# A stencil split in a local part, finished early, and time neighbours, added by transfers

## The reference, cut to what matters

```
x1 = x  + pooled attention over time (masked softmax)                 # stage one
x2 = x1 + zX*(channel neighbours - 2*x1) + zY*(time neighbours - 2*x1) + zR*x1*(1-x1)
   = x1*(1 - 2*(zX+zY) + zR - zR*x1) + zX*(left+right) + zY*(before+after)
x3 = x2 + LayerNorm(x2 + relu(x2 @ Wd + bd) @ Wu + bu) * g + b        # adapter
y  = x3 + LayerNorm((gelu(soma) * sigmoid(temporal)) @ Wout) * gamma + beta
```

## Time and profile before

| what | value |
|---|---|
| median of three runs | 774.7 us (771.69 to 777.08) |
| the profiled execution, its own time | 777.66 us |
| its span, first to last instruction | 775.8 us |
| mean granted clock of TensorE | 0.944 of full |
| busy: PE, DVE, ACT, POOL | 685.9, 552.1, 332.5, 213.3 us |
| moved by DMA | 82.62 MB, mean 106 GB/s |

### The profile page before, as it was taken

One profiled execution on the slowest core, in us unless ns is written; L12 is line 12 of the kernel. 1 busy time (PEld: TensorE's weight loads), 2 busy tenths in 40 slices (PEclk: granted clock), 3 DMA queues, 4 the chain that ended last, 5 costly groups with the idle time before them and its releaser, 6 DMA issues.

```text
span 775.8 us, 7905 instructions
## 1 busy us (share of the span) xinstructions
PE 685.9 (88%) x2808; PEld 503.2 (65%) x2808; DVE 552.1 (71%) x736; ACT 332.5 (43%) x694; POOL 213.3 (27%) x219
## 2 busy tenths in 40 slices
PE   4979398479999979997999799979997999899986
PEld 2445154237778757875787578757775777577874
DVE  3545265674985997599659975987599759875964
ACT  1241136214357235723572356235623661465244
POOL 5004212742324312431243124213421342031001
PEclk9989689689999989998999999989999999899999
DMA  7965858497305170517041805270427050405001
GB/s 223 303 221 175 259 143 266 146 274 228 55 0 109 58 160 1 109 58 160 0 109 58 159 2 108 72 145 1 110 80 138 0 109 1 55 1 109 0 1 55
DMA packets 49829, 82.62 MB, mean 106 GB/s; under 512 B 8176, under 2 KB 10224, under 8 KB 49790
## 3 DMA queue, kind: packets, MB, share of 16 engines
q1 hardware_dynamic: 33630, 56.93, 21.3%
q0 software_dynamic: 12672, 25.17, 20.0%
q10 hardware_dynamic: 3488, 0.01, 0.3%
HBM read 65.31 MB, written 16.79 MB: 106 GB/s over the span
## 4 chain that ended last, share of the span: by engine, by line
PE 57%; DVE 18%; issue 8%; ACT 6%; DMA 5%; POOL 4%; SPq 1%; POOLq 0%; DVEq 0%; ACTq 0%
PE bank L1019 13%; PE bank L1021 13%; PE bank L1020 13%; POOL wide L534 4%; PE bank L1059 4%; PE bank L1075 3%; DVE hb L1444 3%; DVE tr L1465 3%; PE bank L922 3%; DVE xr L1375 2%; DMA wg_l_f<-in_wg 2%; PE bank L1015 2%; PE bank L1084 2%; DVE tr L1459 2%; ACT wide L702 2%
## 5 line engine op out<-in xcount | busy, mean ns | idle before, releaser
L1367 DVE SCALAR_TENSOR_TENSOR nb<-nb,coef,wide 128x2048 f32<-128x2048 f32 x8 | 38.9, 4867 | 44.4 <-POOL wide L534 30.3
L1465 DVE TENSOR_TENSOR_SCAN tr<-alpha,carry,tr 128x512 f32<-128x512 f32 x48 | 58.9, 1268 | 0.0
L584 POOL TENSOR_TENSOR rs_a<-ss_a,consts 128x1 f32<-128x1 f32 x32 | 15.9, 498 | 131.7 <-ACT hb L721 131.6
L1019 PE MATMUL bank<-xh,wg_l 128*128 128x512 f32 x128 | 52.1, 407 | 0.0
L1019 PE MATMUL bank<-th,wg_l 128*128 128x512 f32 x128 | 52.0, 406 | 0.0
L1021 PE MATMUL bank<-xh,wg_h 128*128 128x512 f32 x128 | 50.2, 392 | 0.0
L1021 PE MATMUL bank<-th,wg_h 128*128 128x512 f32 x128 | 50.1, 391 | 0.0
L1020 PE MATMUL bank<-xl,wg_h 128*128 128x512 f32 x128 | 50.1, 391 | 0.0
L1020 PE MATMUL bank<-tl,wg_h 128*128 128x512 f32 x128 | 49.9, 390 | 0.0
L1459 DVE SCALAR_TENSOR_TENSOR tr<-wgb,blend_w,mod 128x512 f32<-128x512 f32 x64 | 45.3, 749 | 3.8 <-ACT mod L747 2.9
L570 POOL DMA_DIRECT2D xr<-rows_scratch x16 | 23.5, 1466 | 77.5 <-PE bank L1084 55.9
(11 more groups left out here) (238 smaller groups left out, 1994.9 us busy)
## 6 DMA issues: line engine op xcount, KB each, us to landing
xr<-rows_scratch POOLq DMA_DIRECT2D x16, 1024.0 KB, 10.8
xb<-in_x SPq DMA_DIRECT2D x8, 1024.0 KB, 14.5
x_scratch<-xb SPq DMA_DIRECT2D x8, 1024.0 KB, 6.0
nb<-x_scratch SPq DMA_DIRECT2D x8, 1024.0 KB, 5.5
nb<-x_scratch POOLq DMA_DIRECT2D x8, 1024.0 KB, 9.3
x1s<-x_scratch SPq DMA_DIRECT2D x7, 1024.0 KB, 5.6
result<-xr SPq DMA_DIRECT2D x7, 1024.0 KB, 4.3
xb<-in_xT SPq DMA_DIRECT2D x3, 1024.0 KB, 10.4
```

What stands on the lines that cost most here:

```text
L1019: pe.matmul(acc, wl, xh_, start=start, stop=False)
L1367: ve.scalar_tensor_tensor(flat(nb[:]), flat(nb[:]), coef[:, ZY, b:b + 1], flat(wide[:]), ALU.mult, ALU.add).then_inc(mix_t, 1)
L1465: ve.tensor_tensor_scan(t[:, d], alpha[:, 1 + d:2 + d].broadcast_to([P, GN]), t[:, d], 0.0 if first else carry[:, k, 1 + d:2 + d], ALU.mul ...
```

## The change

The stencil is split by linearity. In **stage one**, each of the eight blocks n of 512 steps gets its local part finished as soon as its x1 is there: ScalarE `mix_local(n)` makes the factor in a buffer `local_of(n)`, VectorE `by_local(n)` multiplies it by x1 (this was POOL's `local`), POOL `channels(n)` makes left+right in one buffer `side`, and VectorE `stencil(n)` adds zX times `side`. ScalarE `scale_beside(n)` then multiplies x1 by zY in place, and `store_beside(n)` stores that with one row more on each side; `store_local(n)` stores the local part (the program stores it for blocks 2 to 7, and blocks 0 and 1 stay in `xr`). In **stage two** nothing is mixed. `load_x2(q)` loads the local part, two buffers in turn, and the two time neighbours are added onto it by two accumulating transfers of the POOL queue, `add_before(q)` and `add_after(q)`, the second waiting for the first. `x2_transposes(q)` now waits for `after_add`. `times` is gone.

Moved along with it: 

- `xT` of batch 1 goes into buffers of the gate weights and is loaded with x of batch 1 and `wn1` right behind the first loads, with no wait; the two halves of `wg` are loaded behind `hid_mm` 8, and `wg_hi(0)` no longer stands between `tanh(1, 2)` and `tanh(1, 3)` on ScalarE. It stands behind the evictions of `probT`.
- `pooled` of batch 0 uses three banks in turn, not two. `x2_transposes(0)` stands behind `pooled(1, 1)` (was behind `pooled(0, 12)`), `down(0)` behind `pooled(1, 3)`, `up(0)` behind `pooled(1, 5)`, `x3_transposes(0)` behind `pooled(1, 9)` (was behind `pooled(1, 7)`); `replicate(1)` stands behind `pooled(0, 13)`.
- ScalarE in stage one, after: `tanh(1,1)`, `scale_beside(0)`, `mix_local(1)`, `tanh(1,2)`, `tanh(1,3)`, `scale_beside(1)`, `mix_local(2)`, the softmax's `block_exps(1)` and `prob_exps(1)`, `sums_raw(1)`, `wn1` high, `scale_beside(2)`, `sums_hi(1)`, `bw_evict` and `probT_evict` of batch 1, `mix_local(3)`, `wg_hi(0)`, `scale_beside(3)`, `x2_evict(0)`, `wg_hi(1)`, `relu(0)`, and on as in the diff.
- VectorE in stage one, after: `x1(0, 7)`, `by_local(0)`, `stencil(0)`, `params_a`, `read_scores(1, 0)`, `x1(0, 8)`, `params_b`, `read_scores(1, 1)`, `x1(0, 9)`, `by_local(1)`, `stencil(1)`, `read_scores(1, 2)`, `x1(0, 10)`, `x1(0, 11)`, `read_scores(1, 3)`, `softmax_in(1)`, `x1(0, 12)`, `x1(0, 13)`, `by_local(2)`, `normalise_out(1)`, `x1(0, 14)`, `stencil(2)`, `normalise(1)`, `sums_low(1)`, `x1(0, 15)`, `x1(1, 0)`, `x1(1, 1)`, `by_local(3)`, `stencil(3)`, `x1(1, 2..5)`, `y_sum(0, 0..3)`, `x1(1, 6)`, `x1(1, 7)`, `ln_weigh(0, 0..3)` with `x1(1, 8)` and `x1(1, 9)`, `ln_apply(0, 0..3)`, and on as in the diff.
- In `front(g)` the products CTX of a column block come ahead of PRE. `mod` is halved per d, behind `sigmoid_gate(g, 0)`.
- In group 0, `weight_hi(2)` (`wo`) and `weight_hi(1)` (`wt`) and their low halves on POOL follow within the group; `soma_in(0, 0)` still waits for `w2_lo` 2.

The core of the diff:

```diff
+
+        def x2_of(q):
+            return xr[:, q] if q < 2 else (x2b0, x2b1)[q % 2][:]
...
+            xt_slot = [[xts[:, 0], xts[:, 1], xts[:, 2], as_slot(probT[:])],
+                       [wg_raw[:, 0:KE], wg_raw[:, KE:], wg_st[:, 0:KE], wg_st[:, KE:]]]
+            side = as_tiles(xts[:, 2])
+
+            def local_of(n):
+                return xr[:, n] if n < 2 else as_tiles(xts[:, n % 2])
...
+                    def store_beside(n):
+                        b, j = n // NG, n % NG
+                        sp.wait_ge(beside_done, n + 1)
+                        done = beside_out[b][j]
...
+                    def store_local(n):
+                        sp.wait_ge(local_done, n + 1)
+                        sp.dma_start(local_rows(n), local_of(n)).then_inc(local_out[n], 16)
+
+                    def load_x2(q):
+                        if q == 2:
+                            beside_landed(sp, 0, 0)
+                        elif q == 3:
+                            sp.wait_ge(x1_done, B * NT)
+                            sp.wait_ge(local_done, GROUPS)
+                            sp.wait_ge(beside_done, GROUPS)
                         else:
-                            sp.wait_ge(mix_v, q)
-                            sp.wait_ge(chan, 3 * q)
-                        sp.dma_start(x1s[:], rows_of_x1(b, j, 0)).then_inc(x1s_in, 16)
+                            sp.wait_ge(x3_done, GT * (q - 1))
+                        sp.wait_ge(local_out[q], 16)
+                        sp.dma_start(x2_of(q), local_rows(q)).then_inc(x2_in, 16)
...
+                    def channels(n):
+                        xg = x1_of(n)
+                        po.wait_ge(x1_done, GT * (n + 1))
+                        if n:
+                            po.wait_ge(local_done, n)
+                        po.tensor_tensor(side[:, :, 1:E - 1], xg[:, :, 0:E - 2], xg[:, :, 2:E], ALU.add)\
+                          .then_inc(chan, 1)
+                        po.tensor_scalar(side[:, :, 0:1], xg[:, :, 1:2], 2.0, None, ALU.mult).then_inc(chan, 1)
+                        po.tensor_scalar(side[:, :, E - 1:E], xg[:, :, E - 2:E - 1], 2.0, None, ALU.mult)\
+                          .then_inc(chan, 1)
+
+                    def add_before(q):
+                        b, j = q // NG, q % NG
+                        if q < 2:
+                            po.wait_ge(local_done, q + 1)
                         else:
-                            po.wait_ge(x1s_in, 16 * q)
-                        if q == 1:
-                            po.wait_ge(masks_set, S_MASKS)
-                        elif q > 1:
-                            po.wait_ge(o_out, 16 * (q - 1))
-                        po.tensor_tensor(s[:, :, 1:E - 1], xg[:, :, 0:E - 2], xg[:, :, 2:E], ALU.add)\
-                          .then_inc(chan, 1)
-                        po.tensor_scalar(s[:, :, 0:1], xg[:, :, 1:2], 2.0, None, ALU.mult).then_inc(chan, 1)
-                        po.tensor_scalar(s[:, :, E - 1:E], xg[:, :, E - 2:E - 1], 2.0, None, ALU.mult)\
-                          .then_inc(chan, 1)
+                            po.wait_ge(x2_in, 16 * (q - 1))
+                        beside_landed(po, b, j - 1)
+                        beside_landed(po, b, j)
+                        po.dma_start(x2_of(q), beside_rows(b, j, -1), accum_op=ALU.add).then_inc(before_add, 16)
 
...
                     def add_after(q):
                         b, j = q // NG, q % NG
-                        po.wait_ge(nb_in, 16 * (q + 1))
-                        x1_landed(po, b, j)
-                        x1_landed(po, b, j + 1)
-                        po.dma_start(nb[:], rows_of_x1(b, j, 1), accum_op=ALU.add).then_inc(nb_sum, 16)
+                        po.wait_ge(before_add, 16 * (q + 1))
+                        beside_landed(po, b, j + 1)
+                        po.dma_start(x2_of(q), beside_rows(b, j, 1), accum_op=ALU.add).then_inc(after_add, 16)
...
-                    local(0)
                     channels(0)
+                    channels(1)
+                    add_before(0)
+                    channels(2)
                     add_after(0)
-                    weight_low(0, wg_h[:, 0:KE], wg_l[:, 0:KE], wg_st[:, 0:KE])
+                    weight_low(0, wn1_h[:], wn1_l[:], wn1_st[:])
+                    channels(3)
+                    add_before(1)
                     add_up_bias(0)
-                    weight_low(1, wg_h[:, KE:], wg_l[:, KE:], wg_st[:, KE:])
+                    weight_low(1, wg_h[:, 0:KE], wg_l[:, 0:KE], wg_st[:, 0:KE])
                     add_after(1)
-                    weight_low(2, wn1_h[:], wn1_l[:], wn1_st[:])
+                    weight_low(2, wg_h[:, KE:], wg_l[:, KE:], wg_st[:, KE:])
+                    channels(4)
                     for c in range(GT):
                         rstd(ln_ss, ss_a, EPSILON, rs_a, c, ln_p, ln_rs, c)
-                    local(1)
-                    channels(1)
+                    channels(5)
                     add_shift(0)
-                    weight2_low(1, wo_h[:], wo_l[:], wo_st[:])
-                    add_after(2)
-                    weight2_low(2, ws_h[:], ws_l[:], ws_st[:])
+                    channels(6)
+                    channels(7)
+                    weight2_low(1, ws_h[:], ws_l[:], ws_st[:])
...
+                        if g + 2 < GROUPS:
+                            add_before(g + 2)
+                            if g == 0:
+                                weight2_low(2, wo_h[:], wo_l[:], wo_st[:])
+                            add_after(g + 2)
                         if g < LAST:
                             add_up_bias(g + 1)
+                            if g == 0:
+                                weight2_low(3, wt_h[:], wt_l[:], wt_st[:])
                             for c in range(GT):
...
+                    def mix_local(n):
+                        b = n // NG
+                        act.wait_ge(x1_done, GT * (n + 1))
+                        if n < 2:
+                            act.wait_ge(masks_set, S_MASKS)
+                        elif n >= 4:
+                            act.wait_ge(local_out[n - 2], 16)
+                        act.activation(local_of(n), x1_of(n), ACT.Identity, bias=coef[:, MID, b:b + 1],
+                                       scale=coef[:, NEG_ZR, b:b + 1]).then_inc(mix_u, 1)
+
+                    def scale_beside(n):
+                        b = n // NG
+                        act.wait_ge(mix_v, n + 1)
+                        act.wait_ge(chan, 3 * (n + 1))
+                        act.activation(x1_of(n), x1_of(n), ACT.Identity, scale=coef[:, ZY, b:b + 1])\
+                           .then_inc(beside_done, 1)
...
+                    mix_local(4)
                     for c in range(GT):
                         ln_moments(0, c)
-                    wg_hi(2, wn1_h[:], wn1_st[:])
-                    mix_local(1)
+                    scale_beside(4)
+                    mix_local(5)
                     act.wait_ge(params_set, S_PARAMS)
-                    for j in range(NG):
-                        x1_landed(act, 0, j)
+                    beside_landed(act, 0, 3)
                     x3_evict(0)
-                    weight_hi(2, wo_h[:], wo_st[:])
+                    scale_beside(5)
+                    mix_local(6)
+                    mix_local(7)
+                    scale_beside(6)
                     weight_hi(0, ws_h[:], ws_st[:])
+                    scale_beside(7)
...
-                        if g and adapted:
-                            mix_local(g + 1)
                         n1_gelu(g)
-                        mod_sigmoid(g)
                         keep_ctx(g, 0)
                         sigmoid_gate(g, 0)
-                        add_half(g)
+                        mod_sigmoid(g)
...
+                                pe.wait_ge(x3T_hi, KE * g + 3)
                             elif k == 1:
-                                pe.wait_ge(o_done, GT * g)
+                                pe.wait_ge(n1_act, g + 1)
                             elif k == 2:
                                 pe.wait_ge(x3T_hi, KE * g + KE)
                             else:
+                                pe.wait_ge(ctx_scan, KE * g + 1)
+                            by_x3(g, bank[CTX[k]][:], wg_h, wg_l, KE, chunk(k)).then_inc(ctx_mm, 1)
+                            if k == 0:
+                                pe.wait_ge(x3T_hi, KE * g + 2)
+                            elif k == 1 and g > 0:
+                                pe.wait_ge(o_done, GT * g)
+                            elif k == 3:
                                 pe.wait_ge(pre_add, KE * g + 1)
                             by_x3(g, bank[PRE[k]][:], wg_h, wg_l, 0, chunk(k)).then_inc(pre_mm, 1)
-                            if k == 0:
-                                pe.wait_ge(x3T_hi, KE * g + 3)
-                            elif k == 3:
-                                pe.wait_ge(ctx_scan, KE * g + 1)
```

(57 more changed lines are left out.)

326 lines of the change are left out of this document (144 added, 182 removed).

## The result

The changed kernel takes 743.8 us (median of 4 runs), the kernel before 773.2 in the same job: ratio 0.962, interval 0.957 to 0.967. The forecast was 736 in a range of 724 to 755. The profiled execution took 746.6 us with a span of 744.8, against 775.8 before.

A forecast was written before the change was run, and what follows sets the result against it. Stage two was held bound by the mixing chain ahead of logits(g, 0), then TensorE; stage one by a string of waits. 777.66 - 43.1 - 1 + 0 + 5.5 = 739.1, or 736 us on the medians' scale, range 724 to 755.

The forecast's parts named there:

- Stage two: Groups 1 to 6, freed of mixing, go from 77.13 to 69.94 us each, 43.1 us less in all.
- B: Rival: stage two keeps a wait of 2 us per group, set by the VectorE chain; +18, 754 us; chance 0.08.
- The exchange of CTX and PRE: In front(g), the first scan can start some 2.7 us earlier, but the add still waits for PRE; costed at nothing.
- The two transfers: POOL's accumulating transfers in stage two: cost nothing with their lead of a group, up to 27 us per group without.
- Last group: Group 7, with mod halved per d: 1 us gained, bounds 0 to 1.5.
- Stage one: Start of front(0) stays at about 171.5 against 172.31: no change, bounds -8 and +13.
- The walk: Some forty steps of stage one followed in the new order, ending with x1(1, 15) at about 171.5.
- Tail and group 0: Last mixing steps, 13.3 us in series on VectorE, make TensorE stand 5 to 7 us before mod: +5.5, bounds 0 and 12.
- A: Rival: stage one grows through the shared side, the port and ScalarE as middleman; +26, 762 us; chance 0.12.
- C: Rival: each stage-one block becomes a closed ring of 12.85 us, making the kernel slower at 789 us; chance 0.03.
- D: Rival: stage one comes out 12 us shorter, the 11.0 and 13.1 us waits both gone; 724 us; chance 0.10.

The follow-up runs named there:

- logits2: Kernel before, on VectorE times(g+1) moved behind logits(g, 1) and logits(g, 2) ahead of traces(g, 1) and trace_lo(g, 0), mixing kept in stage two: 733.6 us, ratio 0.950.
- ctx_first: Kernel before with only CTX made ahead of PRE in front(g): 772.6 us, ratio 1.000.
- swap_back: Changed kernel with PRE ahead of CTX again in front: 748.1 us, ratio 0.968.
- adds_late: Changed kernel with both accumulating transfers of block g+1 issued at the head of group g, without their lead of a group: 744.4 us, ratio 0.963.
- evict_bias: Changed kernel with the order of evict_first and, on POOL, add_up_bias(0) ahead of add_before(1): 742.4 us, ratio 0.960.
- ws_low_late: Changed kernel with POOL's weight2_low(1), the low half of wsoma, waiting until stencil(7) is done: 744.3 us, ratio 0.964.
- evict_first: Changed kernel, ScalarE doing x2_evict(0) ahead of wg_hi(0) and scale_beside(3), and x3_evict(0) ahead of scale_beside(4) and mix_local(5): 741.9 us, ratio 0.959.
- mod_later: The evict_first kernel with the two mod products of group 0 behind PRE[2] in place of PRE[0]: 752.9 us, ratio 0.974.

## Why the prediction was right, and which terms were off

The forecast of 736 us was 7.8 short of the measured 743.8: stage two came out 2 us better, stage one 4 to 6 worse, the tail and group 0 5 worse.

**Stage two, forecast -43.1, measured -45.1.** Mechanism and size held. The floor that I read from group 0, 69.94 us, is 69.62; TensorE is busy in all of it at clock 1.00. B (a wait stays) is excluded by that row.

**What I had not drawn from it.** I named the chain ahead of `logits(g, 0)` as the limit and took the removal of the mixing as its cure. `logits2` shows that the mixing can stay where it was: two changes of order on VectorE bring the same 69.62. So the 4.7 us of VectorE per group were not the cost; the cost was their place ahead of two deadlines, `logits(g, 0)` and `logits(g, 2)`. In the kernel before, `times` took 5.59 us ahead of the first, and all scans of the group stood behind it.

**The exchange of CTX and PRE, forecast 0.** Right in the kernel before (`ctx_first`, ratio 1.000), and in groups 1 to 6. It has a value outside them: undone in the changed kernel it costs 4 us (`swap_back`), of which 2.5 are placed, in group 0 and the last group; put into `logits2` it gives 3.6.

**The two transfers, forecast 0 with their lead, up to 27 without.** The 0 held. The 27 was wrong by all of it: `adds_late` costs nothing. I had counted the string from the load, which can stay early, and left out the 24 us between POOL's first issue and the transposes.

**Last group, forecast -1, measured -0.7.**

**Stage one, forecast 0 (-8 to +13), measured +4.3, like for like +6.** This step was mis-sized. The walk got the front half: first `probT` eviction 105.55 (forecast 104), end of `scale_beside(3)` 116.9 (117.6). The adapter came later than walked:

```profile
119.95 1.28 POOL L578 DMA_DIRECT2D xr<-rows_scratch  x1 [3.85 <-PE bank L1081]
135.75 0.69 DVE L1452 SCALAR_TENSOR_TENSOR tr<-bank,xr 128x512 f32<-128x512 f32 x1 [6.75 <-DMA xr<-rows_scratch]
152.91 2.00 ACT L719 ACTIVATE xb<-xb,coef 128x2048 f32<-128x2048 f32 x1 [10.81 <-DVE xts L1404]
156.81 0.67 ACT L749 ACTIVATE soma<-bank,shift_cols 128x512 f32<-128x512 f32 x1
```

The bias row landed at 135.7 in place of 131, so `ln_apply(0)` ended at 150.7 in place of 144, and ScalarE stood in `scale_beside(4)` until 152.91 and reached `x3_evict(0)` at 156.8 in place of 150.5. With both of ScalarE's stands removed `front(0)` starts at 170.6 and the kernel is 2 us faster, so they carry part of it. The last `x1` ended at 176.4 (forecast 171.5), and TensorE stood 8.8 us for it ahead of `front(0)`, where I had the 3.5 of before. Why the bias row landed late is in part shown: issued ahead of `add_before(1)` it takes 10.2 us (`evict_bias`).

**Tail and group 0, forecast +5.5 (0 to 12), measured +10.4.** The mechanism held and a term was missing. TensorE waits 6.27 us for `wn_rep` (forecast 5 to 7) with the slow clock behind it: the four `mod` products ran at a granted clock of 0.50, the 1.2 GHz level, in 3.75 us in place of 1.88:

```profile
188.00:194.25 6.25, 0.00 (x0) 0.03 (x1) 6.22 (x4) 3.14 (x3) 4.80 (x2) 0.90 1.01 349
194.25:198.50 4.25, 4.25 (x6) 2.09 (x7) 2.72 (x4) 2.67 (x5) 0.00 (x0) 0.50 1.03 158
```

`mod` came 17.6 us behind `front(0)` against 9.9 before, that is 7.7 of the 10.4: the wait, and 1.4 since the 36 products ahead of it took 11.3 us at a mean granted clock of 0.73, against 9.9 at 0.83 before. The other 2.7 are from `mod` to `x3_transposes(1)`, 51.79 against 49.06; the slow `mod` is 1.9 of it. The Trainium skill's rule (SBUF — State Buffer, "SBUF: two separate sides") that a VectorE instruction with two SBUF inputs and a GpSimd one that reads SBUF exclude each other for a whole instruction is borne out in both directions in the tail, 6.60 us for a VectorE step of 2.35 and 5.50 for a POOL step of 3.6.

What I left out is that POOL's weight half lands in the tail too: over 4 us more in series, on `stencil(7)` here, on the copies in `ws_low_late` and `evict_first`. From the start of `by_local(6)` at 176.3 to the end of the copies at 194.1 the tail took 17.8 us, not the 13.3 that I added up. That the wait still came out at its forecast is luck: I had the 36 products at 8.2 us, and their slow clock hid 3.1 of the 4.5.

A (762) and C (789) did not come: `front(0)` moved by 4 to 6 us, not by 26 or more. I take it that the `pooled` products fill the time between the blocks; no run tests that. D (724) did not come: the wait of 13.1 us is gone and that of 11.0 is down to 5.3, but TensorE now also stands 8.8, 6.6, 5.4 and 5.3 us in stage one.

**Slips in the working.** None changes the forecast. ScalarE's added work is six `mix_local` and eight `scale_beside` of 2.1 us, 29.4 and not 27. The row of 20.88 us is that of group 7; group 0 has 252.21 - 231.29 = 20.92. The DMA share of the group's row is 0.37, not 0.38.

## What to carry to other kernels

When the engine that should be the floor waits in every turn of a loop, list what its supplier does between its last free moment and that delivery, and ask of each step whether the waiting engine needs it. Two changes of order gave 5.0% here (733.6 us) where moving the work to another stage gave 3.8%, since stage one and group 0 gave back some 15 of the 45 us won. And in a stage that is a string of waits, a wait is no gain until the one beneath it is priced. Five kernels here took a stand away in stage one or the tail: one gained 2 us (`evict_first`), three gained nothing, and one lost 11 (`mod_later`).

## What was unexpected of the hardware

- An accumulating transfer of 1 MB takes 10.3 us to landing in stage two, a plain load of the same size 5.5; among other transfers it is slower still. All transfers of the first queue below accumulate, none of the second. The last row is the bias row's stretch, with the DMA engines full at 253 GB/s:

```profile
x2b<-beside_scratch POOLq DMA_DIRECT2D x12, 1024.0 KB, 10.3
x2b<-local_scratch SPq DMA_DIRECT2D x6, 1024.0 KB, 5.5
...
q0 software_dynamic: 16896, 33.56, 27.9%
q1 hardware_dynamic: 32046, 53.79, 21.0%
...
120.00:136.00 16.00, 9.92 (x24) 4.46 (x22) 3.26 (x5) 5.98 (x6) 15.52 (x7) 0.93 1.09 253
```

The row took 15.7 us there. Per MB the accumulating transfers held the 16 engines for 0.83% of the span and the plain ones for 0.39%. So a full DMA is not seen in the GB/s here; the share shows it.
